# Four of the last group's eight transposes move from ahead of the forward transform into the products of the modes

## The reference

```python
x = coords @ fc0_w + fc0_b                     # 3 -> 32 channels
for sw, cw, cb in four_layers:
    x_ft = rfft2(x)[:, :, :20, :20]            # 20 x 20 modes are kept
    out = einsum('bixy,ioxy->boxy', x_ft, sw)  # products of the modes, a 32x32 matrix for each
    x = gelu(irfft2(out) + einsum('bchw,oc->bohw', x, cw) + cb)
x = gelu(x @ fc1_w + fc1_b) @ fc2_w + fc2_b
```

## Time and profile before

| | |
|---|---|
| median of three runs | 6175.48 us (6164.15, 6175.48, 6176.18) |
| the profiled execution | 6138.44 us |
| its span, first to last instruction | 6135.5 us |
| mean granted clock of TensorE | 0.952 |
| TensorE busy | 5481.0 us |
| VectorE, ScalarE, GpSimd busy | 2832.0, 2673.2, 1103.5 us |

### The profile page before, as it was taken

How to read it: one execution, slowest core, us unless ns; L and a number is a source line. 1 busy time by engine, 2 the same in 40 slices (tenths; PEclk the granted TensorE clock), 3 DMA queues, 4 the chain that set the end, 5 groups by cost and what they waited for, 6 DMA issues and landing times. The chain is left out here.

```text
span 6135.5 us, 273892 instructions
## 1 busy us (share of the span) xinstructions
PE 5481.0 (89%) x119157; PEld 4115.8 (67%) x119157; DVE 2832.0 (46%) x4407; ACT 2673.2 (44%) x4998; POOL 1103.5 (18%) x1045
## 2 busy tenths in 40 slices
PE   8999999999899989989988998999999788888888
PEld 6776777678767776877677767776777443434343
DVE  4443444344434443444344434443444474848484
ACT  3335333533353335333533353335334564747473
POOL 4220322032202221222222222212221000000000
PEclk9999999999999999999999999999999798989898
DMA  2111111111111120111012101110110100000000
GB/s 35 14 15 15 20 14 14 17 18 14 14 18 17 14 25 9 15 20 19 10 14 25 14 10 23 16 15 12 20 16 4 22 1 8 1 8 1 4 1 4
DMA packets 442829, 85.51 MB, mean 14 GB/s; under 512 B 437336, under 2 KB 437608, under 8 KB 441544
## 3 DMA queue, kind: packets, MB, share of 16 engines
q1 hardware_dynamic: 439624, 67.23, 8.8%
q10 hardware_dynamic: 2048, 0.53, 0.0%
HBM read 63.51 MB, written 4.23 MB: 11 GB/s over the span
## 5 line engine op out<-in xcount | busy, mean ns | idle before, releaser
L218 POOL COPY x_T<-x_X 128x512 f32<-128x512 f32 x1024 | 1074.4, 1101 | 3565.4 <-ACTq L810 3386.6
L805 ACT ACTIVATE x_X<-ga 128x512 f32<-128x512 f32 x1280 | 751.3, 597 | 1098.7 <-PE ga L469 906.6
L658 DVE COPY x_X<-ev 128x512 f32<-128x512 f32 x640 | 438.3, 688 | 847.8 <-PE ev L488 778.3
L469 PEld LDWEIGHTS ga<-pw_rhs,x_X 64*64 64x64 f32 x32768 | 593.8, 135 | 279.7 <-issue 278.9
L658 DVE COPY V<-ev 104x512 f32<-104x512 f32 x608 | 411.2, 689 | 602.9 <-PE ev L435 444.8
L500 PEld LDWEIGHTS ev<-dft_consts,x_T 128*64 128x64 f32 x16384 | 578.7, 137 | 42.3 <-issue 41.9
L500 PE MATMUL ev<-dft_consts,x_T 128*64 128x80 f32 x16384 | 599.7, 234 | 4.3 <-POOL x_T L218 3.4
L469 PE MATMUL ga<-pw_rhs,x_X 64*64 64x64 f32 x32768 | 585.5, 218 | 5.0 <-issue 4.3
L461 PE MATMUL ga<-V,inv_w 40*64 40x512 f32 x4096 | 549.7, 604 | 29.6 <-ACT V L773 27.9
L658 DVE COPY Y<-ev 128x400 f32<-128x400 f32 (+1 forms) x768 | 462.8, 603 | 211.9 <-PE ev L500 167.5
L658 DVE COPY D<-ev 128x512 f32<-128x512 f32 x576 | 362.1, 684 | 330.7 <-PE ev L407 328.3
(11 more groups left out here) (210 smaller groups left out, 8216.4 us busy)
## 6 DMA issues: line engine op xcount, KB each, us to landing
mix_w<-in_sw SPq DMA_DIRECT2D x128, 400.0 KB
coords<-in_coords SPq DMA_DIRECT2D x66, 96.0 KB, 2.1
maps<-Y SPq DMA_DIRECT2D x128, 16.0 KB
raw<-maps SPq DMA_DIRECT2D x8, 256.0 KB, 3.5
out<-out_t SPq DMA_DIRECT2D x8, 256.0 KB, 3.5
w<-in_w SPq DMA_DIRECT2D x3, 512.0 KB, 6.9
dft_consts<-in_dft ACTq DMA_DIRECT2D x1, 336.0 KB
fc_rhs<-in_fc_w SPq DMA_DIRECT2D x16, 0.4 KB
```

The costliest lines, as they stand in the source:

```text
L218: pool.tensor_copy(x_T[:, :, H * bc + h0:H * bc + h0 + 16].rearrange("p c (s n) -> p c s n", n=2), blocks.rearrange("p (s a n c) -> p a c ...
L469: last = pe.matmul(ps[HALF * bp:HALF * bp + HALF, HALF * s:HALF * s + HALF], x_X[r:r + HALF, g, col:col + HALF], pw_rhs[r:r + HALF, :], st ...
L658: dve.tensor_copy(dst, src).then_inc(ev_taken, 1)
L805: x_new = act.activation(blocks.rearrange("p (s a n) -> p s a n", s=8, a=2)[:, :, bc, :], ga[n % N_GA][:, :].rearrange("p (s n) -> p s n", ...
```

## The change

`turn_x` of group 3 in "first" and "mid" does only the first four tiles, on all engines. The other four stand in `mix_next`: one in each of its four passes, behind the fifth of the ten steps, into a PSUM bank of its own (tile 4 and 6 by VectorE, 5 and 7 by ScalarE). Each pass asks for its own banks when it begins; before, a half of the mix asked for those of both passes at once. The fifth group's products stand behind every step of the second pass. VectorE copies pw_rhs before it waits for the first tile. LATE, which is 2, moves the counts.

```diff
+        LATE = TURN_X // 4
-        MIX_V = MIX_S = MIX_T // 2
+        MIX_V = MIX_S = MIX_T // 2 + LATE
-        EV_FIRST = NG * (TURN_V + FWD_W + FWD_H)
+        EV_FIRST = NG * (TURN_V + FWD_W + FWD_H) - LATE
...
+                    def late_turn(ps, i, signal):
+
+                        for q in range(4):
+                            col = (4 * i + q) * P
+                            last = pe.transpose(ps[:, P * q:P * q + P], x_X[:, NG - 1, col:col + P], ident)
+                        last.then_inc(signal, 1)
+
                     for p in range(2):
-                        pairs = [(ev_tile(), ga_tile()) for _ in range(2)]
-                        third = ev_tile() if p else ga_tile()
-                        passed()
-                        for a, pair in enumerate(pairs):
+                        for a in range(2):
+                            late = ga_tile() if a else ev_tile()
+                            if a:
+                                passed()
+                            pair = (ev_tile(), ga_tile())
+                            if a:
+                                passed()
+                                third = ev_tile() if p else ga_tile()
+                            passed()
                             k0 = MIX_K * a
                             for k in range(MIX_K):
...
-                                if k % 2:
-                                    done = a == 1 and k == MIX_K - 1
-                                    fifth(third, MIX_K * p, (MIX_K * a + k) // 2,
-                                          (ev_ready if p else ga_ready) if done else None)
+                                if k == MIX_K // 2 - 1:
+                                    late_turn(late, TURN_X // 2 + 2 * p + a, ga_ready if a else ev_ready)
+                                if a:
+                                    fifth(third, MIX_K * p, k, (ev_ready if p else ga_ready) if k == MIX_K - 1 else None)
...
-                    turn_x(g)
+                    turn_x(g, range(TURN_X if g + 1 < NG else TURN_X // 2))
...
                 def mix():
-                    for i, (kg, k0) in enumerate([(0, 0), (0, MIX_K), (2, 0), (2, MIX_K), (KG - 1, MIX_K)]):
+                    dve.tensor_copy(pw_rhs[:, :], pw_all[:, bass.ds(layer, 1), :].rearrange("p a n -> p (a n)"))
+                    tiles = [(None, 4, None), (0, 0, 0), (0, MIX_K, 2), (None, 6, None), (2, 0, 4), (2, MIX_K, 6),
+                             (KG - 1, MIX_K, None)]
+                    for kg, k0, other in tiles:
                         ps = ev_tile()
...
+                        if kg is None:
+
+                            take(x_X[:, NG - 1, BC * k0:BC * k0 + BC], ps[:, :])
+                            continue
```

More of the change, by code:

```diff
@@ L160, in fno_program @@
         INV_V = INV_S = INV_T // 2
[L161 removed]
+        LATE = TURN_X // 4
+        MIX_V = MIX_S = MIX_T // 2 + LATE
         TURN_D0 = 3
[L163 to L164 removed]
+        EV_FIRST = NG * (TURN_V + FWD_W + FWD_H) - LATE
+        EV_MID = MIX_V + TURN_D0 + (NG - 1) * TURN_D + NG * (INV_V + TURN_V + FWD_W + FWD_H) - LATE
         EV_LAST = MIX_V + TURN_D0 + (NG - 1) * TURN_D + INV_V + (NG - 1) * INV_T + NG * (TURN_V + 1)
         EV_CHUNK = EV_FIRST + (LAYERS - 1) * EV_MID + EV_LAST
[L167 to L168 removed]
+        GA_FIRST = NG * (NB + TURN_S) - LATE
+        GA_MID = MIX_S + TURN_D - TURN_D0 + NG * (NB + TURN_S + INV_S) - LATE
         G1_T = 16
@@ L660, in mix @@
                 def mix():
-                    for i, (kg, k0) in enumerate([(0, 0), (0, MIX_K), (2, 0), (2, MIX_K), (KG - 1, MIX_K)]):
+                    dve.tensor_copy(pw_rhs[:, :], pw_all[:, bass.ds(layer, 1), :].rearrange("p a n -> p (a n)"))
+                    tiles = [(None, 4, None), (0, 0, 0), (0, MIX_K, 2), (None, 6, None), (2, 0, 4), (2, MIX_K, 6),
+                             (KG - 1, MIX_K, None)]
+                    for kg, k0, other in tiles:
                         ps = ev_tile()
[L663 to L667, removed]
+                        if kg is None:
+                            take(x_X[:, NG - 1, BC * k0:BC * k0 + BC], ps[:, :])
+                            continue
+                        if other is not None:
+                            dve.wait_ge(ga_ready, ga0 + other + 1)
                         z = ps[:, 0:MIX_K * MIX_N].rearrange("p (k b r) -> p b k r", k=MIX_K, r=2)
@@ L751, in run @@
                         continue
-                    turn_x(g)
+                    turn_x(g, range(0, TURN_X if g + 1 < NG else TURN_X // 2, 2))
                     forward_w()
@@ L779, in run @@
                 if kind != "first":
-                    for kg, k0 in [(1, 0), (1, MIX_K), (KG - 1, 0), (3, 0), (3, MIX_K)]:
+                    tiles = [(1, 0, 1), (None, 5, None), (1, MIX_K, 2), (KG - 1, 0, None), (3, 0, 4), (None, 7, None),
+                             (3, MIX_K, 5)]
+                    for kg, k0, other in tiles:
                         act.wait_ge(ga_ready, ga0 + n + 1)
-                        if kg < KG - 1:
-                            act.wait_ge(ev_ready, ev0 + kg // 2 * 2 + k0 // MIX_K + 1)
+                        if kg is None:
+                            act.activation(x_X[:, NG - 1, BC * k0:BC * k0 + BC], ga[n % N_GA][:, :], ACT.Copy)\
+                                .then_inc(ga_taken, 1)
+                            n += 1
+                            continue
+                        if other is not None:
+                            act.wait_ge(ev_ready, ev0 + other + 1)
                         z = ga[n % N_GA][:, 0:MIX_K * MIX_N].rearrange("p (k b r) -> p b k r", k=MIX_K, r=2)
@@ L837, in inverse_h_pair @@
                         return n + 1
-                    for i in range(1, TURN_X, 2):
+                    for i in range(1, TURN_X if kind == "last" or g + 1 < NG else TURN_X // 2, 2):
                         n = turn_x(i)
```

## The result

| | before | after |
|---|---|---|
| median, lowest and highest | 6172.35 (6164.15 to 6176.18), 4 runs | 6232.91 us (6203.59 to 6269.59), 4 runs |
| the profiled execution, its span | 6138.44, 6135.5 us | 6203.59, 6200.1 us |

The ratio of the fast runs on record is 1.0115, with an interval of 1.009 to 1.014: slower by 1.15%. Between the medians in the table lie 61 us (0.98%), between the spans 65 us (1.05%). The changed kernel's runs lie 66 us apart, those of before 12 us.

The account below looks back on a forecast made before the run. TensorE's own work and the gaps in it bound the kernel. Mix growth of 37.6 us, less 1.4 ahead of the forward transform and 10 for the clock, made +26 us on 6175.5: 6202 us, 8-in-10 range 6160 to 6250.

Parts of the forecast that it names:

- the likeliest case: The prediction's own forecast for the whole kernel: slower, 6202 us, with its own range 6180 to 6230 us; chance 0.58.
- Four tiles leave turn_x: Ahead of the forward transform: 1.82 us of TensorE work go, but GpSimd's last copy still holds it; only 1.4 us gained.
- A late tile 0.66 us, four 2.64: In each mix: a transposed tile among small products costs 0.66 us, against 0.456 in a row of tiles; four cost 2.64.
- The stops shrink from 2.33 to about 1 us: Inside a "mid" mix: late tiles fill part of TensorE's waits for instructions, so the mix grows by 1.3 us.
- blocks that arrive one in 4.06 us: In the mix: instruction blocks keep coming one in 4.06 us, so late tiles fill only part of the stops.
- the full-clock sum: Growth of all mixes: 24 "mid" at 1.3 us and 8 "first" at 0.8 us, 37.6 us together.
- The fifth group's products cost nothing: In the mix: moved to the second passes, they remain 20 in each half, one between two steps; nothing is added.
- The clock: -10 us, bounds +20 and -60: At the seams: with shorter stops the high clock holds to the mix's end more often, 0.3 us gained each.
- all exposed: Rival in the mix: the stops stay and the tiles add their full price, +84 us, 6258 us; chance 0.10.
- the clock holds: Rival: tiles keep 2.4 GHz through the mix and the gap behind it, 70 us gained, ending at 6141 us; chance 0.12.

## Why the prediction was right in its direction and short in its size

The time forecast was 6202 us, the range 6160 to 6250; it came to 6232.91, inside the range but above the likeliest case's own 6180 to 6230. The sum was +26 us, the measured difference +61 (+65 in the spans). That it came no further off is partly luck, since the terms missed in opposite directions.

*Four tiles leave turn_x: -1.4 us.* Right. The distance to GpSimd stayed 0.24 us in the mean of the 32 seams, 1.7 us of idle time opened, and the kernel without the tiles gained nothing.

*A late tile 0.66 us, four 2.64.* Right in kind; a tile came 9% dearer, 0.72 us, and four 2.88.

*The stops shrink from 2.33 to about 1 us.* Wrong in its mechanism. In 14 of the 24 mixes that don't fall early they vanished, and in the other ten at most one in a "mid" mix was left; the argument by blocks that arrive one in 4.06 us, whatever the array does, doesn't hold. On the other side the prediction missed a new stop of 0.35 us: "each pass asks for its own banks" was told in the change and costed at nothing, but a request is several instructions of TensorE's sequencer, and no array work covers them between such short products. The errors partly cancel: a "mid" mix grew by 0.89 us (forecast 1.3), a "first" one from 10.80 to about 11.8 us (forecast +0.8), and the full-clock sum is 26 to 29 instead of 37.6 us.

*The fifth group's products cost nothing.* Wrong, and it hides two effects. Their move alone makes the kernel 0.26% faster. But over one execution each, 48 of 256 mixes fell early in the eight profiles with the move, and 6 of 128 in the four with the products spread. Moved in one half only, it was 2 of 32. One of the eight had 3, and so had one of the four. In the clean pair, with the tiles behind the mix, the move costs time: 0.9917 against 0.9863.

*The clock: -10 us, bounds +20 and -60.* This is the term that failed, in sign and beyond its upper bound: +30 to +34 us in the mixes, up to +45 with the rest of the seam. The prediction looked at the stop from which the clock fell in the earlier trace rows and held that filling it would keep the clock up. Late falls did become rare, 2 instead of 17. But falls within the first 3 us, of which the earlier trace rows showed one, went from 1 to 8, and with tiles they are dear. Timeline of such a mix, at 1.2 GHz:

```profile
223.62 0.29 PE L394 MATMUL ga<-S,mix_w 64*64 64x32 f32 x1
223.84 1.11 PE L375 MATMUL ga<-dft_consts,x_X 128*128 128x128 f32 x4
224.88 0.32 PE L366 MATMUL ga<-S,mix_w 64*64 64x32 f32 x2
```

A tile takes 1.26 us there from product to product, four some 5 us; 12.18 us without tiles and 17 with them agree. Before, the low clock cost a mix only 1.7 us, since it ran in place of the stops: 12.18 us and no stop, against 10.46 with 2.33 us of stops. Tiles in that mix have nothing to hide in. The prediction had this sentence in its rival "all exposed" ("the tiles would add twice their price"), with 0.10; it came true for a quarter of the mixes.

*The rival "the clock holds"* was priced at 2.2 us a seam, 70 us, and put aside because the gap behind the mix stays empty. That is just what the experiments fill: with the tiles in the gap, 2.11 us a seam come back, some 0.6 of them from shorter stops in the mix. The Trainium skill ("TensorE: Matmul & The Clock Gate", Part 4: PE-mode transpose) says that the high clock doesn't engage for transposes. The runs disagree: in the timeline behind a mix above, the tiles from 817.62 ran at the low clock with nothing but transposes on the array, 0.81 to 0.85 us each (granted clock 0.52 from 817.62 to 821.20), and turn_d behind them at the high one (1.00 from 821.85 to 824.30), its first tile 0.49 us.

What stays open: why a mix falls early in one seam and not in the next, and why the fifth group's place matters to it, if it does: the counts are from one execution each. The place of the code and the seam's moment in the run both change from kernel to kernel, and no run here separates them.

## What to carry to other kernels

Before work is moved to fill stops, look for the wait that is idle in every execution. Here that was the 2.2 us behind the mix, an engine's copies with nothing else to do, and not the stops inside it, which vary with the clock and, it seems, the place of the code. With the fifth group's products spread, the four tiles cost 0.52% inside the mix, and behind it that kernel gained 1.37%; with these products moved they cost 1.15% and gained 0.83%.

Price moved work at both clock levels, and count how often the trace shows each. Here a mix of small matmuls that waits for instructions took 10.46 us at the high clock and 12.18 at the low one; with four full-size tiles in it, 11.2 and 16.9.

## What the runs showed of the hardware beyond that

In the changed kernel's trace from 500.40 to 500.98 us TensorE's sequencer goes on to the next instruction 0.15 us after each empty instruction, and 0.09 us after each register sum (with which the value of a wait is computed). Beside products that need 0.06 us for four, three such requests are a stop of 0.35 us. The profile puts it down to a VectorE copy that happened to end 0.33 us earlier, while the weight load 0.03 us ahead of it says "issue": the two rows side by side give it away.
